# Storing the split token rows from GpSimd's queue instead of SyncE's

## The reference

```python
xn = _layernorm(x, axis=-1)                       # 4096 tokens x 512
s = _L0_attn_ref(xn, qkv, o_proj, gamma, beta)    # second layernorm, q k v, causal softmax, o_proj, + residual
g = _silu(_L0_ffn_ref(xn, router_w, wg, wu, wd, sg, su, sd))
x = x + s * g
...
gates = softmax(xf @ router_w.T)                  # 8 experts, the two best of each token, renormalised
y_e = _silu(xf @ wg_e) * (xf @ wu_e) @ wd_e       # expert width 352
shared = _silu(xf @ sg) * (xf @ su) @ sd          # shared expert, width 704
```

## Time and profile before

| | before |
|---|---|
| median of 3 runs | 1158.92 us (1158.82 to 1160.46) |
| the profiled execution, its own time | 1158.34 us |
| its span | 1156.6 us |
| TensorE busy | 1132.1 us, 98% of the span |
| VectorE, ScalarE, GpSimd busy | 570.5, 473.5 and 423.4 us |
| SyncE's transfer queue (q1) | 354104 packets, 172.76 MB |
| GpSimd's transfer queue (q0) | 10800 packets, 35.69 MB |

### The profile page before, as it was taken

How to read it: one execution, slowest core, us unless ns; L and a number is a source line. 1 busy time by engine, 2 the same in 40 slices (tenths; PEclk the granted TensorE clock), 3 DMA queues, 4 the chain that set the end, 5 groups by cost and what they waited for, 6 DMA issues and landing times. The chain is left out here.

```text
span 1156.6 us, 21228 instructions
## 1 busy us (share of the span) xinstructions
PE 1132.1 (98%) x6598; PEld 627.3 (54%) x6599; DVE 570.5 (49%) x1236; ACT 473.5 (41%) x859; POOL 423.4 (37%) x656
## 2 busy tenths in 40 slices
PE   8899999999999999999999999998999999999997
PEld 5555555555555555555555555554454444444454
DVE  6866667677468322211221122111377467467467
ACT  5544444444332223322332233224645545654643
POOL 1363333332200122222222222212764764764663
PEclk9999999999999999999999999999999999999999
DMA  9889999989633589989898878776767668766355
GB/s 288 232 190 219 232 233 236 202 220 231 158 71 77 117 170 209 207 198 209 193 203 191 185 173 182 179 169 163 152 163 186 157 160 184 166 161 182 114 150 126
DMA packets 365004, 209.31 MB, mean 181 GB/s; under 512 B 304309, under 2 KB 314817, under 8 KB 364937
## 3 DMA queue, kind: packets, MB, share of 16 engines
q1 hardware_dynamic: 354104, 172.76, 64.7%
q0 software_dynamic: 10800, 35.69, 12.2%
q10 hardware_dynamic: 32, 0.02, 0.0%
HBM read 89.44 MB, written 46.01 MB: 117 GB/s over the span
## 5 line engine op out<-in xcount | busy, mean ns | idle before, releaser
L708 PE MATMUL pair<-arena 128*128 (+2 forms) x3240 | 506.2, 313 | 0.2 <-issue 0.2
L708 PEld LDWEIGHTS pair<-arena 128*128 128x128 f16 x3240 | 316.1, 98 | 182.6 <-issue 0.9
L1629 DVE SCALAR_TENSOR_TENSOR arena<-pair,slot_unit,arena 128x352 f32<-128x352 f32 x71 | 41.4, 583 | 268.8 <-ACT arena L1519 220.3
L715 PE MATMUL bank<-arena 128*128 x639 | 149.3, 379 | 1.3 <-DMA arena<-arena 1.3
L1519 ACT ACTIVATE arena<-pair,slot_unit 128x352 f32<-128x352 f32 x71 | 39.4, 555 | 205.5 <-PE pair L708 172.1
L1238 POOL COPY arena<-token_of 128x1 uint32 (+1 forms) x71 | 13.0, 183 | 271.3 <-issue 103.3
L715 PEld LDWEIGHTS bank<-arena 128*128 128x128 f16 x639 | 62.5, 98 | 67.7 <-issue 1.8
L1910 PE MATMUL pair<-arena 128*128 128x512 f16 (+3 forms) x576 | 97.5, 326 | 0.6 <-ACT arena L1979 0.6
L1923 PE MATMUL bank<-arena 128*128 128x512 f16 x411 | 93.4, 379 | 0.0
L1240 POOL DMA_INDIRECT arena<-xn_rows,arena x71 | 71.4, 1005 | 55.7 <-POOL arena L1238 54.1
L1895 PE MATMUL bank<-arena 128*128 128x512 f16 x384 | 86.0, 379 | 1.6 <-PEq L1058 1.6
(11 more groups left out here) (205 smaller groups left out, 1356.4 us busy)
## 6 DMA issues: line engine op xcount, KB each, us to landing
slot_rows<-arena SPq DMA_DIRECT2D x71, 256.0 KB
arena<-in_L_attn_x_dram SPq DMA_DIRECT2D x64, 256.0 KB, 3.6
xn_rows<-arena SPq DMA_DIRECT2D x32, 260.0 KB, 2.5
shared_rows<-arena SPq DMA_DIRECT2D x32, 256.0 KB
arena<-shared_rows SPq DMA_DIRECT2D x32, 256.0 KB
out_dram<-arena SPq DMA_DIRECT2D x31, 256.0 KB, 2.8
arena<-in_L_ffn_wg_dram SPq DMA_DIRECT2D x32, 176.0 KB, 3.1
arena<-in_L_ffn_wu_dram SPq DMA_DIRECT2D x32, 176.0 KB, 3.4
```

Source lines behind the costliest of these rows:

```text
L708: last = pe.matmul(bank[:, 0:width], xt[:, a, c, :], weights(c, b, col, width), start=(c == 0 and i == 0), stop=(c == KC - 1 and i == 2))
L715: last = pe.matmul(bank[:, :], ht[:, a, c, :], weights(c, b), start=(start and c == 0 and i == 0), stop=(stop and c == HC - 1 and i == 2))
L1629: v.scalar_tensor_tensor(sbuf[u], u_banks[u][:, 0:H], slot_unit[u][:, 1:2], sbuf[u], ALU.mult, ALU.mult).then_inc(slot_h_ready, 1)
```

## The change

The store of each of the 32 split tiles is issued by GpSimd through its own queue, as the last instruction of `x_low`. GpSimd already waited there for the semaphore of its subtraction, so the change adds no wait to it. SyncE's `store_x16` and its 32 calls go, each with its wait for the same semaphore. Bytes, addresses and the semaphore `xn_stored` are as before.

```diff
             pool.tensor_tensor(x16[u][:, D:2 * D], xb[u], x16[u][:, 0:D], ALU.subtract).then_inc(x16_lo, 1)
             pool.wait_ge(x16_lo, t + 1)
+            pool.dma_start(xn_rows[t * P:(t + 1) * P, :].bitcast(U32), x16[u].bitcast(U32)).then_inc(xn_stored[u], 16)
...
-        def store_x16(sp, t):
-            u = t % 2
-            sp.wait_ge(x16_lo, t + 1)
-            sp.dma_start(xn_rows[t * P:(t + 1) * P, :].bitcast(U32), x16[u].bitcast(U32)).then_inc(xn_stored[u], 16)
...
                 turn_x16(sp, 1)
-                for t in range(2):
-                    store_x16(sp, t)
...
                         if t > 1:
                             turn_x(t)
-                            store_x16(sp, t)
```

## The result

| | before | after |
|---|---|---|
| median of 14 runs each, same chip, in turns | 1158.87 us (1156.42 to 1161.71) | 1164.34 us (1161.46 to 1169.54) |
| ratio after / before | | 1.0053, 95% interval 1.0042 to 1.0064 |
| the profiled execution: own time, span | 1158.34, 1156.6 us | 1163.67, 1161.9 us |

The median grew by 5.5 us. The ratio is an estimate over the rounds and not the quotient of the two medians, which is 1.0047. The forecast was 1157.8 us with a range of 1154.6 to 1162.4: wrong in sign, and the result is outside the range.

What follows compares the result with a forecast made beforehand. TensorE bounds the kernel, busy 1132.1 of 1156.6 us; at most 5.2 us of waits could go. Terms of -0.85 and -0.25 sum to -1.1 us: 1157.8 us against the median 1158.92, range 1154.6 to 1162.4.

Steps and rivals of the forecast that it cites:

- What leaves SyncE: On SyncE's queue: each store gone saves 0.62 us, 20 us over 32, counting only where SyncE is what comes late.
- step 3 of the sum: Step of tiles 5 and 6, at 86.61 us: L1114 0.2 us early, all behind it about 0.85 early.
- TensorE at 55.76: First wait for hidden rows: L1114 moves up by 0.62 us, so the wait shrinks from 1.73 to 1.1 us.
- Tile 3 to 4: No cover on GpSimd: +1.0 us for its store, -0.62 on SyncE, so TensorE +0.38 late; wait at 79 over 2 us.
- The cover of 1.98 us: Double steps: 1.98 us between tile 6's subtraction and its transpose, enough to hide a GpSimd store of 1.0, just 1.8.
- The side effect: Double steps: L291 starts 1.0 us later, L1550 falls from 1.09 to 0.25 us, hidden rows ready about 0.6 us earlier.
- no stall: GpSimd's stores: a skill rule's stall by VectorE, 2.5 us extra each, not expected; as a rival 1163 us, chance 0.05.
- the bounds 0.43 to 1.8: Range in us for one store's cost on GpSimd; 1.0 was taken.
- the full gain: All five TensorE waits for the hidden rows' transpose go: -5.2 us, 1153.7 us; half of it, 1156.
- The first rival: Queues share DMA engines: each hidden-row transpose lands 1.2 us later, five waits grow by 6.0 us, 1164 us; chance 0.14.
- five waits: TensorE's waits for transposed hidden rows before 310 us: 1.73, 1.22, 0.31, 1.66 and 0.25 us, 5.2 together.
- L1114 landed later than 3.4 us in the median: Sign that the prediction is wrong: the hidden rows' transpose landing later than 3.4 us in the median.

Runs made afterwards that it cites:

- 8: Changed kernel, but GpSimd stores only the last 32 bytes of each row and SyncE the other 2048 where it did before; 1159.32 us, ratio 1.0001.
- 4: Kernel before, all stores on SyncE, first tile's store moved behind load of x and hidden rows' transpose, second tile's behind its load of x; 1158.62 us, 0.9997.
- 5: Kernel before, with only the 20 stores of single steps moved to GpSimd, right behind their subtraction; 1161.07 us, ratio 1.0021.
- 6: The 20 single-step stores on GpSimd, but from tile 4 on each waits until its tile's own transpose has landed; 1159.8 us, ratio to the kernel before 1.0007.
- 10: Kernel before, with only the first tiles' stores of the six double steps moved to GpSimd; 1160.28 us, ratio 1.0011.
- 2: Kernel before, with only the second tiles' stores of the six double steps moved to GpSimd; 1159.12 us, ratio 0.9999.
- 11: Kernel before, all stores on SyncE but at the end of the step, behind weights and both hidden transposes; 1168.27 us, ratio 1.0072.
- experiment 3: Changed kernel, all 32 stores on GpSimd, but the six second tiles' stores wait until the hidden rows' transpose has landed; 1167.94 us, ratio 1.0066.

## Why the prediction was wrong

**Shown.** The bytes of the store in GpSimd's queue cost the time. With these bytes taken out of that queue and the issuing kept (8), the loss is gone (1.0001), the tile's transpose lands after 3.5 us instead of 4.9, and SyncE's next issue takes 0.43 instead of 1.20. With the order of SyncE changed alone (4), nothing is lost. With the overlap taken out for 16 of 20 stores (5 against 6), the landing of the tile's transpose goes from 4.6 to 3.2 us.

**Not shown** is the whole way from there to TensorE. It waits for hidden rows alone. In the double steps their transpose lands 2.3 us later when both stores go through GpSimd's queue; with only the first ones there (10) it is 0.5, and with only the second ones (2) 0.7. In the single steps it lands as before, and what is lost there (5) presumably comes through what SyncE issues later; no run takes that apart.

By the prediction's own steps:

- **What failed: the saving on SyncE, and a landing taken as unchanged.** "What leaves SyncE" took 0.62 us per store as a pure saving for what stands behind. The saving was real in time of issuing (L302 is gone), but the load of x moved up behind a transpose and beside GpSimd's store. It takes 0.14 us more for the first (0.44 to 0.58, experiment 4) and 0.62 more for the second (0.58 to 1.20). -0.62 + 0.76 = +0.14 us: nothing moves up. The trace of before had no load right behind a transpose, and the price of issuing was taken as a constant of the instruction. The larger part of the loss arises in the double steps, by the landing: the sum moved the hidden rows' transposes and left their landing as it was, at +0. It was +2.3 us in the double steps. In step 3 of the sum L1114 was to be 0.2 us early; it was issued 0.89 late and landed another 2.33 later.
- **TensorE at 55.76.** A shorter wait of 1.1 us was predicted; it was 1.98. The hidden transpose was issued 52.22 - 52.06 = 0.16 us earlier, and the product started 3.80 us after that issue instead of 3.54.
- **Tile 3 to 4.** +1.0 for the store on GpSimd was right (0.95, of which 0.79 reached VectorE). -0.62 behind it was not: from transpose to hidden transpose it was 2.43 us before and 74.78 - 72.20 = 2.58 after. So +0.75 instead of +0.38 at TensorE, and the wait at 79 is 1.86 us, where "over 2" was expected.
- **The double steps.** The cover of 1.98 us for GpSimd did hold. The side effect didn't come: L1550 (now L1543) fell from 1.09 to 0.26 us, as predicted, but L291 started later only to meet the last subtraction, L1546, which now takes 1.18 instead of 0.21, in all six steps. From the first one's start to the last one's end it is 87.47 - 85.75 = 1.72 us, against 86.58 - 84.98 = 1.60 before. Of the 0.84 us I had left 0.24 for what might still meet the last one; it was all of it.
- **Queue contents, and no stall.** q0 has 44.21 - 35.69 = 8.52 MB more, q1 as much less, and GpSimd's stores take 607 to 810 ns: the bounds 0.43 to 1.8 held. No engine is seen waiting for `xn_stored`, and the issue of no store is held beside a busy VectorE. The 3.1 us that the Trainium skill gives under "SBUF — State Buffer", section "SBUF: two separate sides", for a transfer of GpSimd that VectorE shuts out, are not seen on any of the 32.
- **Two slips without effect.** The lower bound of the range, 1154.6, is well past the half way to the full gain that its sentence names (1158.9 - 2.6 = 1156.3). And the first readers of `xn_rows` come at 312.4 us and not at 384: the transposes of the six deferred tiles (L1085) read it too. Their rows were stored 120 us or more before.

**The first rival had part of the mechanism, and its number by luck.** "The queues share the engines, and the transposes land later" gave 1164, and the median is 1164.34. It was given 0.14, on the ground that "the same bytes were ahead of L1114 already". That ground was the second failure. It counts the bytes ahead of one transfer, while the landings got later by bytes beside a transfer, and beside the tile's own transpose there had been none. The rival's number came out right by a different sum: not each hidden-row transpose 1.2 us later and five waits longer by that, but 2.3 later in the six double steps and 0.2 in the others, waits 3.1 us longer in all, and 1.5 us of halved clock. The prediction said that it would be wrong if L1114 landed later than 3.4 us in the median. It landed after 3.7 by the events of the trace, so that sign was right but weak; most of the change is in the six landings of the double steps. The Trainium skill has a rule that I should have weighed: "DMA: Bandwidth & Descriptors", section "Issuing engines are not separate DMA queues", says that another issuing engine saves only the time of the issuer. The trace agrees that no more than the time of the issuer can be saved, and even that was not: from the tile's transpose to that of the hidden rows SyncE took 2.38 us in step 1, against 2.39 before.

**What stays open.**
- Why GpSimd's queue hurts more than ScalarE's. A store is (13360 - 10800) / 32 = 80 packets in q0 and (354104 - 349496) / 32 = 144 in q1, so its packets are larger there (4160 bytes against 2080, besides 16 of 4 bytes in each). It takes more engine time as well: the share of q0 rose from 12.2% of 1156.6 to 15.1% of 1161.9 us, which is 34 us of all 16 engines, where q1 gave back 64.7% of 1156.6 less 62.5% of 1161.9, or 22; in ScalarE's queue it was 2.4% of 1159.5, or 28. The Trainium skill, "DMA: Bandwidth & Descriptors", section "Queues, rings and completion order", says that each DMA engine takes turns between the queues that have work, a whole packet at a time. By that, a store behind the transpose in one queue can't delay it, one in a second queue takes every other turn from it, and larger packets make longer turns. It agrees in order with 3.2, 3.9 and 4.9 us, but no run here changed the size of the packets, and none shows that the packets that the profile counts are those of that rule, so it is argued and not shown.
- Why the parts make less than the whole: 20 singles (+0.21%), six firsts (+0.11%) and six seconds (-0.01%) sum to 0.31%, and all 32 cost 0.53%. With half widths of 0.10, 0.13, 0.09 and 0.11% the difference of 0.22 may be partly chance. The landings of the hidden rows speak for more than chance: in the double steps they are 0.5 and 0.7 us later for the parts and 2.3 for the whole. The clock's fall behind a long wait would also make a whole dearer than its parts; that wasn't tried.
- The 0.8 us behind 405 us.
- No version beat the kernel before: 2 and 4 are within the measurement of it.

## What to carry to other kernels

A transfer that leaves a queue doesn't leave the memory system. Before moving one to another engine's queue, ask which latency-critical transfer it will now run beside, and look at landing times, above all of transposes, rather than at the time of issuing saved. The time that an issue takes isn't a property of the instruction either: here the same load took 0.44, 0.58 or 1.20 us by what was under way. And a store that nobody reads for 80 us belongs where nothing urgent is in flight: after the transpose rather than beside it, but before its buffer is wanted again (6 for the landing of the transpose, and 11 for the buffer).

## What the runs showed of the hardware

- The token tiles' transpose landed after 3.2 us with no store in a second queue, 3.9 beside 260 KB of store in ScalarE's queue, and 4.9 beside the same store in GpSimd's (medians of 32).
- SyncE's direct issue right behind that transpose took 0.58 (experiment 4), 0.74 and 1.20 us in these cases, and 0.44 behind another direct transfer (medians).
- One store in GpSimd's queue before or after the hidden rows' transpose made it land 0.5 or 0.7 us later, one on each side of it 2.3 us (means of six double steps).
- A plain store from GpSimd holds it for 0.65 us and leaves 0.30 idle ahead of it, whether it moves 260 KB or 4 KB.
- Behind a wait of 2.53 us TensorE's granted clock was 0.50 for some 3 us, so that the wait cost 4 us rather than 2.5. The clock also fell behind waits of 2.10, 3.86 and 4.13 us, and not behind this one, of 2.75 us, in the trace of experiment 3. The prediction's rivals priced their waits without this.

```profile
211.61 2.12 PE L1307 MATMUL bank<-arena 128*128 128x512 f16 x9 [2.75 <-DMA arena<-arena]
```
